# The prologue of a three-stage decoder block: new orders on VectorE and ScalarE, and the first batch's latents split by these two engines from two PSUM banks

## The chip, the core and the metric

One core of one Trainium2 chip runs the whole program in one launch. Its engines run unsynchronized and wait for each other on semaphores: TensorE (PE; its weight loads are the column PEld), VectorE (DVE), ScalarE (ACT), GpSimd (POOL), and SyncE (SP), which issues most DMAs. Each takes its instructions strictly in the order in which the program lists them. The metric is the device time of one execution, in microseconds (us); lower is better.

## The reference, cut to what matters

Inputs are x, 16 batches of 256 tokens by 256 features, and a context of 16 by 77 by 256. Three blocks follow each other, each with a residual and a plain layer norm:

```
x = LN(x + mixer(x))           # h = x@in_w+b; causal conv of 4 taps; silu; xp = h@xp_w+b
                               # a = exp(-exp(xp[:16])); b = silu(xp[16:]) * sum(h)
                               # state = state*a + b, scanned over 256 tokens; out = state@out_w+b
x = LN(x + xattn(ctx, x))      # ln = LN(x)*g+b;  q = ln@Wq;  k, v = concat(LN(ctx)*g+b, ln)@Wkv
                               # 8 heads of 128; softmax over 77+256 keys; out = heads@Wo + bo
x = LN(x + experts(x))         # top 2 of 8 experts, capacity 512 each, 256 -> 512 -> 256
```

All is float32. A product that needs more precision than one pass gives is made from operands split in a rounded high part (`_hi`) and the rest (`_lo`): three matmuls, hi·lo, lo·hi and hi·hi (helper `three`, L611 to L613).

## The kernel before

The first stage treats the 16 batches one after the other, in a loop over 8 heads in which the mixer, the norms and the projections of the neighbouring batches are laid between the attention steps of this one. The second stage runs the experts. What is changed is the prologue: the function `first()` of each engine (its name on PE, ACT, DVE, POOL and SP), which fills the pipeline before batch 0. All orders are written out by hand; every wait is a semaphore with a constant. There is no planner.

In the prologue:

- SP loads the inputs: x transposed for batches 0 and 1 (`xts`, `full`), weights, and eight weight chunks of 128x1024 (`staged(c)`): chunks 0, 1 are the value weights, 2, 3 the key weights, 4, 5 the query weights, 6, 7 the output weights.
- **Weight splits.** ACT makes w_hi of every chunk (`split_hi`, L1172). w_lo of chunks 0, 1, 2, 4, 5 is DVE's (`split_lo`, L1657, semaphore w_lo_set, counting to 5), that of 3, 6, 7 POOL's (L2025, wk_lo_set).
- **The gated values' chain of batch 0.** PE `in` (L713), ACT eviction and first tap (L1076, L1124), DVE's three other taps (L1447), ACT tanh (`tanh_half`, L1165), DVE `silu` (L1458), PE `xp` (L719), ACT's four steps of `xp` (L1081 to L1087), DVE gate (L1417, L1421) and `scan` (L1495), ACT `state_hi` and DVE `state_lo` (the states split in a row block each), PE `op` (L725), DVE `mixed` (xa = x + mixer, L1526, with its statistics), POOL `powers` (L1994, inverse roots), DVE `latents` (lnp, L1546), PE `ln` (4 transposes, L743).
- **Latents.** ACT `ln` scales and shifts both halves k of the transposed latents out of one bank into `full` (L1103). Half 1 is rounded and its rest taken by DVE (`latents_hi`, L1552, L1386), half 0 by POOL (`latents_part`, L2002, L2004). kvl_set 2 says that both low parts are there.
- **Context.** Tiles of 128 context rows: DVE statistics (`context_stats`), POOL `context_norm` (x_rs L1980, cxn L1983), PE `cT` (2 transposes, L731), ACT cfull (L1096), DVE `context_hi` (L1488), POOL `context_lo` (L1989), then values `vc` (PE, ACT L1091, DVE). Tiles 0 and 1 are in the prologue.
- **Constants.** PE sums Wo's value biases (`value_bias`, L773) and bo (L805) into a bank, DVE copies it (`cvec`, L1705). oww_x is out_w in high and low rows.
- **Idle turns** (L779) are transposes of the identity into an unused bank that keep PE at work.
- After that PE makes k (needs kvl_set 2), q (needs w_lo_set 5, so the low parts of chunks 0, 1, 2, 4, 5), `vc` 1 of tile 1, v, and enters the loop with the scores of head 0.

PE's order around the places concerned is

```
xp | vc 0, vc 1 of tile 0 | cT of tile 1 | value_bias 0-2 | op | value_bias 3-7, bo |
14 idle turns | ln | vc 0 of tile 1 | k | q | vc 1 of tile 1 | v | scores of head 0
```

An instruction that waits holds back all that stands behind it on its engine.

Of the kernel before, what the change touches and what calls it, by code (L numbers as in the profile page):

```python
# [22 lines left out]
ALU = mybir.AluOpType  # L23
# [65 lines left out]
def build(nc, x, xT, ctxt, in_w, xp_w, out_w, vecs, vec16, Wq, Wkv, Wo, bo, emb, W1, W2, out):  # L89
# [8 lines left out]
    with top:  # L98
# [306 lines left out]
        def ap(t):  # L405
            return t.bitcast(F32)
# [201 lines left out]
        def _(pe):  # L608
# [167 lines left out]
            def idle_turns(n, bank):  # L776

                for _ in range(n):
                    pe.transpose(ps[:, bank, 0:P], ident[:], ident[:])  # L779

            def first():
                pe.wait_ge(const_set, 1)
                idle_turns(13, AVB)
                pe.wait_ge(inw_ld, 16)
                unit("in", 0, 0, 0, ps[:, 5, :])
                unit("in", 1, 0, 0, ps[:, 7, :])
                unit("cT", 0, 0, 0, ps[:, 6, :])
                unit("in", 0, 1, 0, ps[:, 0, :], full)
                unit("in", 1, 1, 0, ps[:, 1, :], full)
                pe.wait_ge(xpw_set, 2)  # L790
                idle_turns(22, WOB)
                unit("xp", 0, 0, 0, ps[:, 2, :])
                pe.wait_ge(w_lo_set, 2)
                pe.wait_ge(hp_set, 3)
                unit("vc", 0, 0, 0, ps[:, 0, :])
                unit("vc", 1, 0, 0, ps[:, 4, :])
                pe.wait_ge(cxf_set, 1)
                unit("cT", 0, 1, 0, ps[:, 6, :])
                pe.wait_ge(bvb_set, 1)
                value_bias(range(0, 3))  # L800
                pe.wait_ge(owx_set, 5)
                unit("op", 0, 0, 0, ps[:, 5, :])
                value_bias(range(3, H))
                pe.wait_ge(small_ld, 48)
                pe.matmul(ps[:, AVB, 0:D], ap(ones[0:1, :]), bor[:], start=False, stop=True).then_inc(cvec_mm, 1)  # L805
                pe.wait_ge(hp_set, 4)
                idle_turns(14, S0 + 1)
                pe.wait_ge(cxf_set, 2)
                unit("ln", 0, 0, 0, ps[:, 6, :])
                pe.wait_ge(inp_set, 1)  # L810
                unit("vc", 0, 1, 0, ps[:, 2, :])
                pe.wait_ge(hp_set, 2)
                pe.wait_ge(zero_set, 1)
                pe.wait_ge(wk_lo_set, 1)
                pe.wait_ge(w_lo_set, 3)
                unit("k", 0, 0, 0, ps[:, 7, :])
                pe.wait_ge(xa_set, 1)
                pe.wait_ge(w_lo_set, 5)
                unit("q", 0, 0, 0, ps[:, 5, :])
                pe.wait_ge(vcl_set, 2)  # L820
                unit("vc", 1, 1, 0, ps[:, 4, :])
                pe.wait_ge(kl_set, 1)
                unit("v", 0, 0, 0, ps[:, 7, :])
                pe.wait_ge(hp_set, 4)
# [222 lines left out]
        def _(act):  # L1047
# [112 lines left out]
            def tanh_half(b, u):  # L1160

                a = b + 1
                need(act, cv_set, 4 * a + 2 * u + 2)
                need(act, xp_mm, a)
                act.activation(th[:, 2 * u:2 * u + 2, :], cv[:, 2 * u:2 * u + 2, :], ACT.Tanh,  # L1165
                               scale=0.5).then_inc(th_set, 1)
# [8 lines left out]
            def state_hi(b):  # L1175
                need(act, ys_set, b + 2)
                need(act, op_mm, b + 1)
                for row in (0, 64):
                    act.activation(ys_x[row:row + NST, :], ys[:], ACT.Copy).then_inc(ysh_set, 1)  # L1179

            def first():
                act.wait_ge(const_set, 1)
                act.activation(warm[:], powm[:], ACT.Exp)
                act.wait_ge(bq_set, 1)
                act.wait_ge(zero_set, 1)
                for u in range(2):
                    unit("in", u, 0, 0, ps[:, 5 + 2 * u, :])
                    first_tap(0, u)
                unit("cT", 0, 0, 0, ps[:, 6, :])
                split_hi([0])  # L1190
                tanh_half(-1, 0)
                split_hi([1])
                tanh_half(-1, 1)
                split_hi([2, 3])
                unit("in", 0, 1, 0, ps[:, 0, :])
                act.wait_ge(small_ld, 48)
                unit("xp", 0, 0, 0, ps[:, 2, :])
                unit("in", 1, 1, 0, ps[:, 1, :])
                state_hi(-1)
                unit("vc", 0, 0, 0, ps[:, 0, :])  # L1200
                unit("vc", 1, 0, 0, ps[:, 4, :])
                unit("cT", 0, 1, 0, ps[:, 6, :])
                split_hi([4, 5])
                first_tap(1, 0)
                first_tap(1, 1)
                unit("ln", 0, 0, 0, ps[:, 6, :])
                split_hi([6])
                unit("vc", 0, 1, 0, ps[:, 2, :])
                unit("k", 0, 0, 0, ps[:, 7, :])
                split_hi([7])  # L1210
                unit("q", 0, 0, 0, ps[:, 5, :])
                unit("vc", 1, 1, 0, ps[:, 4, :])
                unit("v", 0, 0, 0, ps[:, 7, :])

            first()
# [168 lines left out]
        def _(dve):  # L1384
            def minus(dst, src, hi):
                return dve.tensor_tensor(dst, src, ap(hi), ALU.subtract)  # L1386
# [265 lines left out]
            def split_lo(chunks):  # L1652
                for c in chunks:
# [3 lines left out]
                    dve.scalar_tensor_tensor(out=w_lo[o], in0=staged(c), scalar=1.0 if which else QSCALE,  # L1657
                                             in1=ap(w_hi[o]), op0=ALU.mult, op1=ALU.subtract).then_inc(w_lo_set, 1)

            def first():  # L1660
                dve.wait_ge(vec_ld, 16)

                dve.tensor_scalar(vec[:, V_BQ:V_BQ + H], vec[:, V_BQ:V_BQ + H], QSCALE, None, ALU.mult).then_inc(bq_set, 1)
                dve.memset(hp[:, :, 0:TAPS - 1], 0.0)
                dve.memset(ap(pT_lo[64:96, 2, :]), 0.0).then_inc(pad_set, 1)
                for i in range(2):
                    for part in (kv_hi[i], kv_lo[i]):
                        last = dve.memset(ap(part[:, :, KEYS:KCOL]), 0.0)
                last.then_inc(zero_set, 1)
                context_stats(0)  # L1670
                dve.wait_ge(xpr_ld, 16)
                dve.memset(xpw[:], 0.0).then_inc(xpw_set, 1)
                dve.wait_ge(xpw_set, 1)
                dve.tensor_copy(xpw[:, :, 0:NST], xpr[:, :, 0:NST])
                dve.tensor_copy(xpw[:, :, 32:32 + NST], xpr[:, :, NST:2 * NST])
                dve.memset(xpw[:, :, 64:80], 1.0).then_inc(xpw_set, 1)
                dve.wait_ge(owx_set, 2)
                dve.memset(ap(ys_x[0:32, :]), 1.0)
                dve.memset(ap(ys_x[64:96, :]), 1.0).then_inc(owx_set, 1)
                for u in range(2):  # L1680
                    for k in range(1, TAPS):
                        tap(0, 2 * u, k)
                        tap(0, 2 * u + 1, k)
                silu(0, 0)
                context_hi(0)
                context_stats(1)
                silu(0, 1)
                split_lo([0, 1])
                dve.wait_ge(oww_ld, 48)
                dve.wait_ge(owx_set, 3)  # L1690
                dve.tensor_copy(oww_x[:], oww[:]).then_inc(owx_set, 1)
                dve.wait_ge(owx_set, 4)
                minus(oww_x[64:96, :], oww[64:96, :], oww_x[64:96, :]).then_inc(owx_set, 1)
                unit("xp", 0, 0, 0, ps[:, 2, :])
                scan(-1, 1, 0)
                split_lo([2])
                state_lo(-1, 1)
                mixed(-1, 1, 0, ps[:, 5, :])
                unit("vc", 0, 0, 0, ps[:, 0, :])
                unit("vc", 1, 0, 0, ps[:, 4, :])  # L1700
                context_hi(1)
                latents(-1, 1, 0)
                split_lo([4])
                dve.wait_ge(cvec_mm, 1)
                dve.tensor_copy(cvec[:], ps[:, AVB, 0:D]).then_inc(cvec_set, 1)  # L1705
                latents_hi(-1, 1, 0)
                split_lo([5])
                unit("k", 0, 0, 0, ps[:, 7, :])
                unit("vc", 0, 1, 0, ps[:, 2, :])
                unit("q", 0, 0, 0, ps[:, 5, :])  # L1710
                dve.wait_ge(w_lo_set, 5)
                dve.memset(ap(v_lo[64:96, 2, :]), 0.0).then_inc(pad_set, 1)
# [244 lines left out]
        def _(pool):  # L1957
# [69 lines left out]
            def first():  # L2027
# [13 lines left out]
                pool.wait_ge(initr_set, 1)  # L2041
                pool.iota(initr[:, :, D], [[P, ST]], NTOK, 1, allow_small_or_imprecise_dtypes=True).then_inc(initr_set, 1)
                context_lo(0)
                context_norm(1)
                pool.wait_ge(ysl_set, 1)
                split_lo([3])
                powers(0)
                context_lo(1)
                latents_part(-1, 1)
                normalised(-1, 1)  # L2050
                split_lo([6, 7])

# [183 lines left out]
```

## Time and profile before

| what | us |
|---|---|
| median of 3 runs (lowest, highest) | 1027.61 (1026.38, 1028.1) |
| the profiled execution | 1027.42 |
| its span, first to last instruction | 1025.7 |
| PE busy in the span | 979.9 (96%) |
| DVE, ACT, POOL busy | 809.4, 729.3, 568.7 |

The span is what the trace covers; the execution's own time is 1.7 us longer. In the trace, a start is counted from the span's start, and a duration runs from an instruction's start to its end. On one engine the next instruction can start some 0.08 us before the end of the one before, so that distances between starts are a little shorter than durations. Matmuls are pipelined: their distances, not their durations, say how fast they run.

### The profile page before, as it was taken

The numbers are of one execution on the slowest core, as the hardware profiler recorded it, in microseconds if no ns is written. First come the engines' busy times: TensorE is split into PE (matmuls) and PEld (weight loads), VectorE is DVE, ScalarE is ACT, GpSimd is POOL, SyncE is SP. The second block draws the span as 40 slices with busy tenths as digits, with TensorE's granted clock in tenths as the row PEclk, the third lists the DMA queues.
The fourth block names the chain that finished last, engine by engine and source line by source line (L and its number), as shares of the span: only waits on it lengthen the run. The fifth ranks groups of instructions, "written<-read, shape, count | busy, mean of one in ns | idle before, by whom it ended". The sixth has DMA issues, their size and how long they took to land.

```text
span 1025.7 us, 21471 instructions
## 1 busy us (share of the span) xinstructions
PE 979.9 (96%) x7018; PEld 929.5 (91%) x7018; DVE 809.4 (79%) x2040; ACT 729.3 (71%) x1865; POOL 568.7 (55%) x967
## 2 busy tenths in 40 slices
PE   8999999999999999999999999999999999999960
PEld 7799999999999999999999999999999999899960
DVE  6887878887888888888888888878887877655526
ACT  6686868787777777776877787868786766365536
POOL 4743464656566556554656566545656463526543
PEclk9999999999999999999999999999999999999985
DMA  7643031213111311113110311041105110386448
GB/s 248 220 135 110 6 118 36 61 35 108 47 50 46 101 53 51 45 59 96 51 45 30 125 51 46 17 137 50 47 11 171 33 41 11 140 293 126 67 60 315
DMA packets 63829, 89.60 MB, mean 87 GB/s; under 512 B 14932, under 2 KB 44680, under 8 KB 63720
## 3 DMA queue, kind: packets, MB, share of 16 engines
q1 hardware_dynamic: 56040, 75.51, 22.8%
q0 software_dynamic: 7680, 12.72, 5.8%
q8 instruction: 58, 0.95, 0.4%
q14 instruction: 51, 0.42, 0.1%
HBM read 49.21 MB, written 38.99 MB: 86 GB/s over the span
## 4 chain that ended last, share of the span: by engine, by line
PE 77%; ACT 8%; DVE 6%; issue 3%; DMA 3%; POOL 1%; SPq 0%; ACTq 0%; DVEq 0%; POOLq 0%
PE ps L611 20%; PE ps L612 20%; PE ps L613 20%; PE ps L640 7%; PE ps L719 3%; DVE nmx L1800 2%; DMA accd<-yo,tku 1%; ACT fx L1378 1%; PE ps L655 1%; PE ps L757 1%; PE ps L657 1%; POOL accd L2174 1%; ACT hp L1076 1%; ACT ys_x L1179 1%; ACT prob L1237 1%
## 5 line engine op out<-in xcount | busy, mean ns | idle before, releaser
L2085 POOL TENSOR_SCALAR prob<-prob,rinv 128x333 f32<-128x333 f32 x256 | 144.4, 575 | 242.1 <-DVE rinv L1809 241.1
L1232 ACT ACTIVATE oT_hi<-ps 128x256 fp32r<-128x256 f32 x126 | 48.5, 385 | 151.4 <-PE ps L657 151.4
L611 PE MATMUL ps<-kv_lo,w_hi 128*128 128x256 f32 (+1 forms) x512 | 154.4, 302 | 1.1 <-DVE kv_lo L1386 1.1
L613 PE MATMUL ps<-kv_hi,w_hi 128*128 128x256 f32 (+1 forms) x512 | 153.4, 300 | 0.0
L612 PE MATMUL ps<-kv_hi,w_lo 128*128 128x256 f32 (+1 forms) x512 | 153.1, 299 | 0.0
L1237 ACT ACTIVATE prob<-ps,nmx 128x333 f32<-128x333 f32 x256 | 135.0, 538 | 7.4 <-DVE nmx L1800 7.4
L1386 DVE TENSOR_TENSOR pT_lo<-ps,pT_hi 128x512 fp32r<-128x512 f32 x254 | 131.8, 550 | 1.1 <-ACT pT_hi L1249 0.3
L1800 DVE TENSOR_REDUCE nmx<-ps 128x2 f32<-128x666 f32 x128 | 108.3, 846 | 9.3 <-PE ps L613 7.9
L640 PE MATMUL ps<-ident,prob 128*128 128x128 f32 (+1 forms) x768 | 105.5, 272 | 1.8 <-POOL prob L2085 1.0
L611 PEld LDWEIGHTS ps<-kv_lo,w_hi 128*128 128x128 f32 x512 | 96.9, 189 | 1.6 <-issue 1.5
L612 PEld LDWEIGHTS ps<-kv_hi,w_lo 128*128 128x128 f32 x512 | 96.5, 189 | 0.0
L613 PEld LDWEIGHTS ps<-kv_hi,w_hi 128*128 128x128 f32 x512 | 96.6, 189 | 0.0
L640 PEld LDWEIGHTS ps<-ident,prob 128*128 128x128 f32 (+1 forms) x768 | 90.1, 140 | 6.2 <-issue 1.6
L1447 DVE SCALAR_TENSOR_TENSOR cv<-hp,vec,cv 128x256 f32<-128x256 f32 x192 | 87.7, 475 | 1.8 <-ACT cv L1124 1.8
L611 PE MATMUL ps<-k_lo,q_hi 128*128 128x334 f32 x256 | 81.0, 317 | 1.9 <-DVE k_lo L1392 1.9
L1392 DVE SCALAR_TENSOR_TENSOR k_lo<-ps,vec,k_hi 128x334 fp32r<-128x334 f32 x128 | 71.6, 559 | 12.2 <-ACT k_hi L1055 11.7
L612 PE MATMUL ps<-k_hi,q_lo 128*128 128x334 f32 x256 | 81.0, 317 | 0.0
L613 PE MATMUL ps<-k_hi,q_hi 128*128 128x334 f32 x256 | 80.6, 315 | 0.0
L611 PE MATMUL ps<-w_lo,oT_hi 128*128 128x256 f32 x254 | 77.5, 305 | 0.2 <-DVE oT_lo L1386 0.2
L2174 POOL DMA_INDIRECT accd<-yo,tku x32 | 52.4, 1637 | 45.4 <-ACT yo L1322 20.0
L1249 ACT ACTIVATE pT_hi<-ps 128x512 fp32r<-128x512 f32 x127 | 77.1, 607 | 0.4
L1972 POOL DMA_INDIRECT slots<-xrow,slot_u x60 | 63.4, 1057 | 21.4 <-issue 20.3
(308 smaller groups left out, 3284.6 us busy)
## 6 DMA issues: line engine op xcount, KB each, us to landing
wraw<-in_W SPq DMA_DIRECT2D x14, 512.0 KB, 7.9
vcd_hi<-vst_hi SPq DMA_DIRECT2D x10, 512.0 KB, 2.7
vcd_lo<-vst_lo SPq DMA_DIRECT2D x10, 512.0 KB, 3.5
v_hi<-vcd_hi SPq DMA_DIRECT2D x32, 154.0 KB
v_lo<-vcd_hi SPq DMA_DIRECT2D x32, 154.0 KB
slots<-initr SPq DMA_DIRECT2D x8, 520.0 KB, 7.8
xs<-in_x SPq DMA_DIRECT2D x16, 256.0 KB, 4.4
xts<-in_xT SPq DMA_DIRECT2D x15, 256.0 KB, 4.1
```

Of the source, the lines that this page charges most:

```text
L611: pe.matmul(dst, hi1, lo2, start=first, stop=False, skip_group_check=True)
L612: pe.matmul(dst, lo1, hi2, start=False, stop=False, skip_group_check=True)
L613: return pe.matmul(dst, hi1, hi2, start=False, stop=last, skip_group_check=True)
L640: last = pe.transpose(ps[0:r, far if j == 2 else T0, (j % 2) * S + t * P:(j % 2) * S + t * P + P], prob[:, ring, t, j * P:j * P + r], iden ...
L1237: act.activation(prob[:, h % 2, t, 0:KEYS], ps[:, S0 + t, 0:KEYS], ACT.Exp, bias=nmx[:, h % 2, t:t + 1], accum_out=rsum[:, h % 2, t:t + 1] ...
L1249: act.activation(pT_hi[:, 0:2, :].rearrange("p j s -> p (j s)"), ps[:, T0, :], ACT.Copy).then_inc(pTh_set, 1)
L1386: return dve.tensor_tensor(dst, src, ap(hi), ALU.subtract)
L1392: dve.scalar_tensor_tensor(out=k_lo[:, idx % 2, :], in0=g[:, 0:KCOL], scalar=vec[:, V_BK + idx:V_BK + idx + 1], in1=ap(k_hi[:, idx % 2, :] ...
L1447: op = dve.scalar_tensor_tensor(out=cv[:, ct, :], in0=hp[:, ct, k:k + S], scalar=w, in1=cv[:, ct, :], op0=ALU.mult, op1=ALU.add)
L1800: dve.tensor_reduce(nmx[:, h % 2, :], ps[:, S0:S0 + NT, 0:KEYS], AX.X, ALU.max, negate=True).then_inc(nmx_set, 1)
L1972: pool.indirect_dma_start(slots, bass.IndirectOffsetOnAxis(slot_u[:, 2 * t + c:2 * t + c + 1], 0), rows[:, t, :], None).then_inc(sc_done, 16)
L2085: pool.tensor_scalar(prob[:, h % 2, t, 0:KEYS], prob[:, h % 2, t, 0:KEYS], rinv[:, h % 2, t:t + 1], 1.0, ALU.mult, ALU.mult).then_inc(norm ...
```

## The change

PE, ACT, DVE and POOL get other orders in `first()`; the latents of batch 0 get functions of their own. Half 0 of the transposed latents goes to bank 6, half 1 to bank 1. ACT makes the high part of each half directly out of its bank. DVE makes `full` of each half out of the same bank, half 1 first, and both low parts. Semaphores keep the two engines from reading one bank at the same time: DVE reads bank 1 first and ACT bank 6, then they change.

```diff
 PE first():
+            def first_latents():
+                pe.wait_ge(lnp_set, 2)
+                for k in range(KD):
+                    for t in range(NT):
+                        last = pe.transpose(ps[:, 6 - 5 * k, t * P:(t + 1) * P],
+                                            lnp[:, t, k * P:(k + 1) * P], ident[:])
+                last.then_inc(ln_mm, 1)
                 unit("vc", 1, 0, 0, ps[:, 4, :])
-                pe.wait_ge(cxf_set, 1)
-                unit("cT", 0, 1, 0, ps[:, 6, :])
                 pe.wait_ge(bvb_set, 1)
                 value_bias(range(0, 3))
...
                 pe.matmul(ps[:, AVB, 0:D], ap(ones[0:1, :]), bor[:], start=False, stop=True).then_inc(cvec_mm, 1)
+                pe.wait_ge(cxf_set, 1)
+                unit("cT", 0, 1, 0, ps[:, 6, :])
                 pe.wait_ge(hp_set, 4)
-                idle_turns(14, S0 + 1)
+                idle_turns(10, S0 + 1)
                 pe.wait_ge(cxf_set, 2)
-                unit("ln", 0, 0, 0, ps[:, 6, :])
+                first_latents()
 ACT first():
+            def first_latents():
+                act.wait_ge(ln_mm, 1)
+                act.wait_ge(zero_set, 1)
+                for k in range(KD):
+                    if k:
+                        act.wait_ge(kvh_set[1], 1)
+                    act.activation(kv_hi[0][:, k, 0:S], ps[:, 6 - 5 * k, 0:S], IDN,
+                                   bias=vec[:, V_BL + k:V_BL + k + 1],
+                                   scale=vec[:, V_GL + k:V_GL + k + 1]).then_inc(lnf_set, 1)
                 tanh_half(-1, 0)
+                tanh_half(-1, 1)
                 split_hi([1])
-                tanh_half(-1, 1)
-                split_hi([2, 3])
                 unit("in", 0, 1, 0, ps[:, 0, :])
+                split_hi([2])
...
                 state_hi(-1)
+                split_hi([3])
...
                 split_hi([4, 5])
-                first_tap(1, 0)
-                first_tap(1, 1)
-                unit("ln", 0, 0, 0, ps[:, 6, :])
+                first_latents()
                 split_hi([6])
                 unit("vc", 0, 1, 0, ps[:, 2, :])
+                first_tap(1, 0)
                 unit("k", 0, 0, 0, ps[:, 7, :])
                 split_hi([7])
                 unit("q", 0, 0, 0, ps[:, 5, :])
                 unit("vc", 1, 1, 0, ps[:, 4, :])
+                first_tap(1, 1)
 DVE first():
+            def first_latents():
+                dve.wait_ge(ln_mm, 1)
+                for k in (1, 0):
+                    if k == 0:
+                        dve.wait_ge(lnf_set, 1)
+                    dve.tensor_scalar(full[:, k, 0:S], ps[:, 6 - 5 * k, 0:S], vec[:, V_GL + k:V_GL + k + 1],
+                                      vec[:, V_BL + k:V_BL + k + 1], ALU.mult, ALU.add).then_inc(kvh_set[k], 1)
+                for k in (1, 0):
+                    dve.wait_ge(kvh_set[k], 1)
+                    dve.wait_ge(lnf_set, k + 1)
+                    minus(kv_lo[0][:, k, 0:S], full[:, k, 0:S], kv_hi[0][:, k, 0:S]).then_inc(kvl_set, 1)
                 silu(0, 0)
                 context_hi(0)
-                context_stats(1)
                 silu(0, 1)
                 split_lo([0, 1])
-                (wait for oww; oww_x copy, oww_x minus)
                 unit("xp", 0, 0, 0, ps[:, 2, :])
                 scan(-1, 1, 0)
-                split_lo([2])
+                context_stats(1)
                 state_lo(-1, 1)
                 mixed(-1, 1, 0, ps[:, 5, :])
                 unit("vc", 0, 0, 0, ps[:, 0, :])
                 unit("vc", 1, 0, 0, ps[:, 4, :])
                 context_hi(1)
                 latents(-1, 1, 0)
-                split_lo([4])
+                split_lo([2])
                 cvec
-                latents_hi(-1, 1, 0)
-                split_lo([5])
+                first_latents()
+                split_lo([4, 5])
                 unit("k", 0, 0, 0, ps[:, 7, :])
 POOL first():
                 context_lo(0)
+                (wait for oww; oww_x copy, oww_x minus, wait for both)
                 context_norm(1)
                 pool.wait_ge(ysl_set, 1)
                 split_lo([3])
                 powers(0)
                 context_lo(1)
-                latents_part(-1, 1)
                 normalised(-1, 1)
                 split_lo([6, 7])
```

Lines in brackets, and the line cvec, stand for the instructions that they name.

## Rows read from the trace of the kernel before

**Rows 1.** Busy time by stretch: us, then busy (instructions) of each engine, PEclk, DMA
```profile
46.00:48.00 2.00, 1.43 (x9) 1.06 (x8) 2.00 (x6) 1.96 (x6) 1.47 (x3) 1.00 1.05 337
...
60.00:80.00 20.00, 19.29 (x136) 18.24 (x135) 15.71 (x39) 16.87 (x44) 12.09 (x14) 1.00 0.16 44
...
993.50:994.00 0.50, 0.00 (x0) 0.00 (x0) 0.00 (x0) 0.00 (x0) 0.20 (x1) 0.82 0.00 0
```

**Rows 2.** Timeline of PE: start, us, line, operation, out<-in, count [idle before <-releaser]
```profile
17.17 1.95 PE L719 MATMUL ps<-th,xpw 128*80 128x256 f32 x8 [1.21 <-DVE th L1458]
...
22.30 0.38 PE L731 MATMUL ps<-ident,cxn 128*128 128x128 f32 x2
...
23.64 0.57 PE L725 MATMUL ps<-oww_x,ys_x 96*128 96x256 f32 x2
...
26.30 0.69 PE L805 MATMUL ps<-bor,ones 1*128 1x256 f32 x2
...
28.82 0.63 PE L743 MATMUL ps<-ident,lnp 128*128 128x128 f32 x4
...
31.95 0.39 PE L611 MATMUL ps<-kv_lo,w_hi 128*128 128x334 f32 x1 [1.11 <-DVE kv_lo L1386]
...
32.96 0.33 PE L611 MATMUL ps<-kv_lo,w_hi 128*128 128x256 f32 x1
...
37.21 0.32 PE L611 MATMUL ps<-k_lo,q_hi 128*128 128x334 f32 x1
```

**Rows 3.** Timeline of DVE in the prologue
```profile
9.79 4.94 DVE L1447 SCALAR_TENSOR_TENSOR cv<-hp,vec,cv 128x256 f32<-128x256 f32 x12 [1.76 <-ACT cv L1124]
...
16.43 0.68 DVE L1458 SCALAR_TENSOR_TENSOR th<-th,cv 128x512 f32<-128x512 f32 x1
17.03 2.35 DVE L1657 SCALAR_TENSOR_TENSOR w_lo<-staging,w_hi 128x1024 fp32r<-128x1024 f32 x2
...
21.25 0.68 DVE L1495 TENSOR_TENSOR_SCAN ys<-dec,inp 16x256 f32<-16x256 f32 x1
...
24.25 0.69 DVE L1526 TENSOR_TENSOR xa<-ps,xs 128x512 f32<-128x512 f32 x1 [0.75 <-PE ps L725]
...
27.32 0.28 DVE L1488 CAST cx_hi<-cfull 128x256 fp32r<-128x256 f32 x1
27.52 1.15 DVE L1546 TENSOR_SCALAR lnp<-xa,a_mv,a_rs 128x256 f32<-128x256 f32 x2
28.59 1.21 DVE L1657 SCALAR_TENSOR_TENSOR w_lo<-staging,w_hi 128x1024 fp32r<-128x1024 f32 x1
29.73 0.41 DVE L1705 COPY cvec<-ps 128x256 f32<-128x256 f32 x1
...
31.62 1.21 DVE L1657 SCALAR_TENSOR_TENSOR w_lo<-staging,w_hi 128x1024 fp32r<-128x1024 f32 x1
```

**Rows 4.** Timeline of ACT in the prologue
```profile
15.10 0.62 ACT L1165 ACTIVATE th<-cv 128x512 f32<-128x512 f32 x1
...
23.82 0.81 ACT L1096 ACTIVATE cfull<-ps,vec 128x128 f32<-128x128 f32 x2
```

**Rows 5.** Timeline of POOL in the prologue
```profile
23.58 2.38 POOL L2025 TENSOR_TENSOR w_lo<-staging,w_hi 128x1024 fp32r<-128x1024 f32 x1 [3.06 <-DVE ys_x L1386]
26.29 1.02 POOL L1994 TENSOR_TENSOR a_rs<-a_vv,powm 128x4 f32<-128x4 f32 x1 [0.34 <-DVE a_vv L1538]
...
31.41 3.65 POOL L2012 TENSOR_SCALAR x<-xa,a_mv,a_rs 128x256 f32<-128x256 f32 x2
```

**Rows 6.** Single tiles: count, duration in ns least/median/most, first and last start
```profile
L1980 POOL TENSOR_TENSOR x_rs<-x_vv,powm x10: 551/578/955, 6.8 to 739.2; 128x1 f32<-128x1 f32 x10
L1983 POOL TENSOR_SCALAR cxn<-cxs,x_mv,x_rs x10: 1213/1236/2785, 7.5 to 740.0; 128x256 f32<-128x256 f32 x10
...
L1386 DVE TENSOR_TENSOR kv_lo<-full,kv_hi x16: 646/648/849, 30.9 to 825.2; 128x256 fp32r<-128x256 f32 x16
...
L1103 ACT ACTIVATE full<-ps,vec x32: 553/560/567, 29.5 to 819.9; 128x256 f32<-128x256 f32 x32
```

More of the change, by code:

```diff
@@ L1685, in first @@
                 context_hi(0)
-                context_stats(1)
                 silu(0, 1)
                 split_lo([0, 1])
[L1689 to L1693, printed above, removed]
                 unit("xp", 0, 0, 0, ps[:, 2, :])
                 scan(-1, 1, 0)
-                split_lo([2])
+                context_stats(1)
                 state_lo(-1, 1)
@@ L2043, in first @@
                 context_lo(0)
+                pool.wait_ge(oww_ld, 48)
+                pool.wait_ge(owx_set, 3)
+                pool.tensor_copy(oww_x[:], oww[:]).then_inc(owx_set, 1)
+                pool.wait_ge(owx_set, 4)
+                pool.tensor_tensor(oww_x[64:96, :], oww[64:96, :], ap(oww_x[64:96, :]),
+                                   ALU.subtract).then_inc(owx_set, 1)
+                pool.wait_ge(owx_set, 5)
                 context_norm(1)
```

## Prediction

> **What bounds the kernel now.** I read busy time by stretches first [rows 1]: in the batches TensorE (PE) is at work for 19.29 of 20 us, the next engine for 16.87, so the prologue moves the end only by when it lets PE go on. The change touches only the prologue, the first 38 us. PE's rows there [rows 2] show the two places where it stood for lack of data: xp at 17.17, which waited for the gated values (silu, 16.43 + 0.68 [rows 3]), and k at 31.95, which waited for the low parts of the latents. From k on PE ran without a hole: q at 32.96, vc 1 of tile 1, v, the first scores at 37.21, and from there the batches. So the question is narrow: when does q start. It needs the low parts of weight chunks 0, 1, 2, 4 and 5, all from VectorE (DVE); the last ends at 31.62 + 1.21 = 32.83 [rows 3] and q starts at 32.96. That wait is hidden, because k ends at about the same moment; it is the one to watch.
>
> The profiled execution took 1027.42 us, 1.7 more than its span of 1025.7; the median of three is 1027.61. A shift in the span goes one for one into both; I put it on the median.
>
> **Part 1: the gated chain.** tanh 1 no longer stands behind the split of chunk 1 on ScalarE (ACT). It needs the last tap, 9.79 + 4.94 = 14.73 [rows 3], and takes 0.62 [rows 4]: ends 15.4 instead of 15.72. On DVE the statistics of context 1, which with their wait for a DMA held silu 1 until 16.43, are gone from in front of it: silu 1 starts at 15.45. Gain 0.98, and xp on PE, its four ACT steps, gate and scan move by as much: scan from 21.25 to 20.27 [rows 3]. DVE is free for them: splits 0 and 1 (2.35, now 16.06 to 18.4) start early by the same 0.98, and the oww pair (0.8 between 19.30 and 20.12) goes to POOL, which has over 3 us of slack for it. vc 0 of tile 0, which waited for split 1 (17.03 + 2.35 = 19.38 [rows 3]), starts at 18.45 for 19.44.
>
> On PE cT of context 1 (22.30 [rows 2]; two transposes, some 0.2 until the biases began) leaves the place ahead of the value biases: the op matmuls move from 23.64 to 22.44. They need the low state: DVE now puts the context statistics (20.87 to 21.71) ahead of it, so it ends at 22.05, in time. Their loads are no wait: the biases ahead of them, which began at 22.5 without one, read the load queued last. So xa starts at 23.05 for 24.25 [rows 3], and the attention norm's variances are out at 25.0 for 26.2: **1.2 us gained.**
>
> **Part 2: where that gain goes.** lnp (the latents before scaling) needs two more things in DVE's queue and POOL's.
> (a) context_hi(1) stands ahead of it and needs cT(1). PE now issues that after cvec: cvec's matmul moves from 26.30 to 25.10 and takes 0.69, so cT is at 25.73 to 26.11; ACT's pair (0.81 [rows 4]) ends at 26.98, where before it ended at 24.63 and nobody waited. DVE stands from 26.2 to 27.03, then 0.20 of cx_hi: lnp at 27.23.
> (b) POOL's powers. Context norm 1 can now start only at 21.8 (x_rs 0.55, cxn 1.21 when undisturbed [rows 6]), ending 23.7; split 3 behind it takes 2.38, to 26.05, and powers 1.02 [rows 5]: ready at 27.08. Disturbed by DVE, x_rs took 0.95, which would put lnp at 27.5.
> So lnp starts at 27.23 for 27.52: of 1.2 us 0.3 are left. The first latents' transposes follow at 28.5 for 28.82 [rows 2]. The idle turns (10 for 14, 0.125 each) end at 27.2 and hide nothing.
>
> **Part 3: the new latents on DVE, and q.** From lnp's start at 27.23, by distances between starts in [rows 3]: 1.07 to split 2 (formerly at 21.86, beside ACT's work, now here), 1.14 to cvec, 0.33 to the first new one, full[1] from PSUM at 29.77. No row has it; I take cvec's 0.41, the same 128x256 from PSUM. ACT's high part of k=1 follows it (the order by kvh_set and lnf_set), 0.56 [rows 6] with 0.04 for each handover: lo[1] can start at 30.82. DVE makes full[0] meanwhile. Then lo[1] and lo[0], both on DVE. The kv_lo row [rows 6] has 0.65 in the median of 16 and 0.85 at 31 us, with POOL at work beside it; a 128x256 from PSUM takes 0.41. I take 0.65: the second ends at 30.82 + 0.57 + 0.65 = 32.04, against 31.70 before. k follows 0.25 later, at 32.3: **0.3 late.**
> Behind them come **both** query splits, 4 and 5, where before only 5 was left: 31.96 + 1.14 + 1.21 = 34.31, and q at 34.44 for 32.96. **+1.48.** With undisturbed low parts (0.42) it is 33.98, +1.02; with 0.85, +1.85; x_rs disturbed adds 0.3. k (about 1 us) ends near 33.3, so PE then stands for 1.1 us.
>
> Edits that I cost at nothing: split_hi 3 behind state_hi (its only user, POOL, takes it at 23.7; it is out at 22.8); first taps of batch 1 behind vc (DVE takes them at about 42; v's eviction may come a little late, hidden behind the first maximum); POOL's latents gone, so that x1 and splits 6, 7 start up to 3 us earlier, where nobody waits. If DVE's splits hold POOL up instead, that lead is what covers it; without it each us more would hold up the first normalisation of batch 0, for which POOL was ready only half a us ahead. On SP, the store of tile 0's values comes 1 us earlier, and next_context(2), the first v loads and the clearing writes, which wait for split 5 or the memset behind q_lo, come later with q; what needs them is later as well.
>
> After q nothing waits: from 34.44 on all PE rows keep their distances and the first scores come at 38.7. Forecast: **+1.5, 1029.1 us.**
>
> **A rule weighed.** POOL's x1 used to start at 31.41; it now starts right behind context_lo(1), at 28.2, just before DVE's split 2. The pair to compare is x1 at 31.41 and split 5 at 31.62 [rows 3, 5], 0.2 behind it: the split took 1.21, as the undisturbed one at 28.59, and x1 took 3.65 for two. So DVE went first and POOL paid. The Trainium skill (SBUF — State Buffer, Who interferes with whom) says that a VectorE instruction with two SBUF inputs and a GpSimd instruction that reads SBUF exclude each other, and that the one issued first blocks the other for its whole length. By that, split 2 would stand until x1's first half is over. The trace agrees that they exclude each other, but not on who pays.
>
> **Rivals.**
> A. Batch 0 takes it back, and a little more (not slower). PE has holes there that hang on DVE's queue: 0.57 in 46 to 48 us and 0.71 in 60 to 80 [rows 1]. If ACT and POOL, which enter the batch less loaded, close both, 1.28, the end is +1.48 − 1.28 = +0.2, and with undisturbed low parts (+1.02) −0.3: 1027.3. It decides from where the holes closed add up to more than q's delay. Against it: the hole at 46.3 lies behind DVE's own taps, whose list is unchanged. 0.17.
> B. POOL holds DVE up: x1's first half, (3.65 − 1.21) / 2 = 1.22, keeps split 2 waiting for 1.1, and lnp's successors with it: +2.6, 1030.2. It decides from where the first half of x1 is issued ahead of split 2. For it: DVE's kv_lo at 31 us took 0.85 where its median is 0.65 [rows 6]. Against it: split 5 at 31.62. 0.17.
> C. TensorE's clock. At 46 to 48 us, with its hole, the granted clock is 1.00 (2.4 GHz), and behind the hole of 1.1 before k the matmuls keep their pace [rows 1, 2]. The last matmul is at 991.8; in the half microsecond from 993.5 the grant is 0.82 [rows 1], a fall to 0.50 (1.2 GHz) at about 993.8, so after 2.0 us without work. PE will stand 1.3 at 27.2, 1.7 at 30.6 and 1.1 at 33.3 with little between. If the clock falls to 1.2 GHz there, the work from q to the first scores (37.21 − 32.96 = 4.25) can take up to twice as long: up to 4.25 on top; I take 2.5, so 1031.6. For it: three holes in 7 us are more than in any stretch before. Against it: none is as long as 2.0. 0.08. The Trainium skill (TensorE: Matmul & The Clock Gate, Part 1) speaks for it: by it the array runs at half rate unless it has lately been kept busy.
> D. The gain of part 1 survives: lnp does come near 26.3 since cT or powers are early in a way that the queues don't show, and q at 33.5, +0.5, 1028.1. 0.05.
> Forecast, with its own range from +0.8 to +2.1 (1028.4 to 1029.7): 0.53.
>
> **How the numbers follow.** What a measurement can tell from no change is about 0.2%, 2.06 us; the forecast is below that. Slower by more: all of C, three quarters of B, an eighth of the forecast's own case: 0.08 + 0.12 + 0.07, 0.27. Faster by more: only the far end of A and what the three times of before leave open (they lie 1.7 apart): 0.09. Same: 0.64. Range 1026.7 to 1031.5: A's better end to C's middle.
>
> **What would show it.** Right: xa near 23.0; cT(1) on ACT at 26.2 and a hole on DVE before cx_hi; powers ending near 27.1; lnp at 27.2; k at 31.8 to 32.4; a hole of 1 us on PE before q, q waiting for a w_lo of DVE at 34.0 to 34.8; first scores at 38.2 to 39. Wrong: xa not before 24 (part 1 fails); lnp before 26.8 (part 2); q before 33.5 or its wait gone (part 3); split 2 starting 1 us after lnp's end (B); L611 matmuls of q at 0.24 distance instead of 0.12 (C); scores 1.5 late but the end not (A).

## The result and the profile after

| | before | changed |
|---|---|---|
| median of 4 runs each (lowest, highest), us | 1027.86 (1026.38, 1028.27) | 1034.3 (1033.73, 1035.27) |
| changed / before, 95% interval | | 1.0064 [1.0052, 1.0075] |
| the profiled execution, us | 1027.42 | 1035.27 |
| its span | 1025.7 | 1033.5 |
| PE busy; DVE, ACT, POOL busy | 979.9; 809.4, 729.3, 568.7 | 982.2; 811.7, 730.0, 575.4 |

The change costs 6.4 us. A second set of six runs against its own runs of before gave 1034.63 to 1027.85, 1.0069 [1.0056, 1.0081]. The prediction was +1.5 (1029.1, range to 1031.5): too low by 5, and outside its range.

The first silu on DVE starts between 13.44 and 14.91 us in the thirteen traces of this document, and the whole prologue moves with it. (TensorE's first `in` begins between 4.88 and 5.34 in them and takes 3.72 to 5.22.) So below, "from silu 0" is the distance to the start of that silu (14.64 before, 14.29 in the changed kernel), which stands ahead of all that was changed.

| from silu 0, us | before | forecast | changed |
|---|---|---|---|
| xa | 9.61 | 8.41 | 9.19 |
| lnp | 12.88 | 12.59 | 13.39 |
| first transpose of the latents (`ln`) | 14.18 | 13.86 | 14.68 |
| k | 17.31 | 17.7 | 18.61 |
| q | 18.32 | 19.80 | 23.96 |
| first scores | 22.57 | 24.06 | 30.96 |

Two steps carry 7.1 of the 8.4 us: k to q (1.01 before, 5.35 now) and q to the scores (4.25, now 7.00). The timeline of PE in the changed kernel (columns as in [rows 2], to which these lines answer):

```profile
15.84 1.95 PE L719 MATMUL ps<-th,xpw 128*80 128x256 f32 x8 [0.23 <-DVE th L1479]
18.84 0.50 PE L611 MATMUL ps<-w_lo,cx_hi 128*128 128x512 f32 x1 [1.05 <-DVE w_lo L1678]
...
26.16 0.44 PE L731 MATMUL ps<-ident,cxn 128*128 128x128 f32 x2
...
28.97 0.63 PE L786 MATMUL ps<-ident,lnp 128*128 128x128 f32 x4 [1.28 <-DVE lnp L1567]
...
32.90 0.39 PE L611 MATMUL ps<-kv_lo,w_hi 128*128 128x334 f32 x1 [1.90 <-DVE kv_lo L1407]
...
38.25 0.55 PE L611 MATMUL ps<-kv_lo,w_hi 128*128 128x256 f32 x1 [4.20 <-issue]
39.03 0.41 PE L611 MATMUL ps<-kv_lo,w_hi 128*128 128x256 f32 x1
...
45.25 0.32 PE L611 MATMUL ps<-k_lo,q_hi 128*128 128x334 f32 x1
```

The view puts the 4.20 ahead of q down to "issue", that is, it found no releaser. The timeline of DVE names it: q needs all five low parts, and the two splits behind the low latents took 5.59 us where two take 2.35 [rows 3]. They end at 38.15, 0.1 ahead of q.

```profile
23.48 0.69 DVE L1547 TENSOR_TENSOR xa<-ps,xs 128x512 f32<-128x512 f32 x1 [1.43 <-PE ps L725]
...
25.21 1.03 DVE L1558 TENSOR_SCALAR a_vv<-a_mv 128x2 f32<-128x2 f32 x1
...
27.68 1.14 DVE L1567 TENSOR_SCALAR lnp<-xa,a_mv,a_rs 128x256 f32<-128x256 f32 x2
28.75 1.21 DVE L1678 SCALAR_TENSOR_TENSOR w_lo<-staging,w_hi 128x1024 fp32r<-128x1024 f32 x1
...
31.89 0.76 DVE L1407 TENSOR_TENSOR kv_lo<-full,kv_hi 128x256 fp32r<-128x256 f32 x2 [0.69 <-ACT kv_hi L1197]
32.56 5.59 DVE L1678 SCALAR_TENSOR_TENSOR w_lo<-staging,w_hi 128x1024 fp32r<-128x1024 f32 x2
```

The timeline of POOL, with x1's two halves and its two last splits in a row each, says what ran beside them:

```profile
15.26 1.11 POOL L2017 TENSOR_TENSOR cx_lo<-cfull,cx_hi 128x256 fp32r<-128x256 f32 x1 [5.20 <-DVE cx_hi L1509]
16.33 1.38 POOL L2074 CAST oww_x<-oww 96x256 fp32r<-96x256 f32 x1
...
23.88 2.35 POOL L2053 TENSOR_TENSOR w_lo<-staging,w_hi 128x1024 fp32r<-128x1024 f32 x1
26.39 1.03 POOL L2022 TENSOR_TENSOR a_rs<-a_vv,powm 128x4 f32<-128x4 f32 x1 [0.17 <-DVE a_vv L1559]
...
28.66 2.31 POOL L2040 TENSOR_SCALAR x<-xa,a_mv,a_rs 128x256 f32<-128x256 f32 x1
...
30.97 1.22 POOL L2040 TENSOR_SCALAR x<-xa,a_mv,a_rs 128x256 f32<-128x256 f32 x1
...
32.27 1.51 POOL L2044 TENSOR_TENSOR x<-x,cvec 128x512 f32<-128x512 f32 x1
33.75 3.33 POOL L2053 TENSOR_TENSOR w_lo<-raw,w_hi 128x1024 fp32r<-128x1024 f32 x1
...
37.03 3.35 POOL L2053 TENSOR_TENSOR w_lo<-raw,w_hi 128x1024 fp32r<-128x1024 f32 x1
```

and DVE's splits 0, 4 and 5, for 1.21 undisturbed [rows 3], with the gate that stands behind split 1:

```profile
15.70 1.76 DVE L1678 SCALAR_TENSOR_TENSOR w_lo<-staging,w_hi 128x1024 fp32r<-128x1024 f32 x1
...
18.83 0.82 DVE L1438 SCALAR_TENSOR_TENSOR gt<-th,ut 16x256 f32<-16x256 f32 x1
...
32.56 2.30 DVE L1678 SCALAR_TENSOR_TENSOR w_lo<-staging,w_hi 128x1024 fp32r<-128x1024 f32 x1
...
34.79 3.36 DVE L1678 SCALAR_TENSOR_TENSOR w_lo<-staging,w_hi 128x1024 fp32r<-128x1024 f32 x1
```

Read them as one queue for a single thing. Split 4 stands until POOL's sum of x1 is over at 33.78, then runs its 1.1 to 34.86. POOL's split 6 (2.4 by itself) stands until then and runs to 37.1; DVE's split 5 stands behind it and runs to 38.15; POOL's split 7 stands behind that and runs to 40.4. Each pays for the one before.

Last, busy time by stretch of the changed kernel (columns as in [rows 1]):

```profile
28.00:30.00 2.00, 1.03 (x7) 0.97 (x8) 2.00 (x4) 1.70 (x3) 2.00 (x2) 1.00 0.84 342
30.00:32.00 2.00, 0.99 (x5) 0.47 (x3) 1.31 (x4) 1.42 (x3) 2.00 (x2) 1.00 0.45 182
32.00:34.00 2.00, 1.10 (x6) 0.92 (x6) 2.00 (x3) 1.76 (x4) 1.92 (x3) 1.00 0.02 4
34.00:36.00 2.00, 0.06 (x1) 0.00 (x0) 2.00 (x2) 1.49 (x2) 2.00 (x1) 0.51 0.00 0
36.00:44.00 8.00, 5.75 (x20) 5.10 (x21) 4.89 (x6) 1.09 (x3) 4.38 (x2) 0.50 0.16 49
44.00:46.00 2.00, 2.00 (x11) 1.77 (x10) 0.12 (x1) 1.88 (x4) 0.00 (x0) 0.93 0.30 104
```

The granted clock is 0.50 (1.2 GHz of 2.4) from 34.0 to about 44.2, so q, vc 1 and a part of v run at half speed: the matmuls of q behind its first took 0.41 (39.03 above) and stood 0.21 apart, for 0.28 and 0.12 at full clock.

### The profile page after: what moved, and what is told of

Its sections match the earlier page's. It is cut to its first block, busy times and chain, and to the rows that moved or that the text cites. A ratio compares the mean times of both kernels' runs of the same rounds, so it can differ in the third digit from the quotient of the medians.

```text
span 1033.5 us, 21467 instructions
## 1 busy us (share of the span) xinstructions
PE 982.2 (95%) x7014; PEld 931.6 (90%) x7014; DVE 811.7 (79%) x2040; ACT 730.0 (71%) x1865; POOL 575.4 (56%) x967
## 4 chain that ended last, share of the span: by engine, by line
PE 73%; ACT 8%; DVE 6%; issue 6%; POOL 4%; DMA 3%; SPq 0%; ACTq 0%; DVEq 0%; POOLq 0%
PE ps L611 19%; PE ps L612 18%; PE ps L613 18%; PE ps L640 7%; POOL accd L2208 4%; DMA accd<-yo,tku 3%; PE ps L719 3%; DVE nmx L1828 1%; ACT fx L1399 1%; PE ps L655 1%; PE ps L657 1%; PE ps L757 1%; ACT hp L1085 1%; ACT ys_x L1188 1%; DVE cv L1468 1%
## 5 line engine op out<-in xcount | busy, mean ns | idle before, releaser
L1421 DVE SCALAR_TENSOR_TENSOR q_lo<-ps,vec,q_hi 128x256 fp32r<-128x256 f32 x128 | 55.8, 477 | 26.8 <-ACT q_hi L1072 26.8
```

## The experiments

**Theory.** Three things add up: DVE's longer queue ahead of q (the forecast's +1.5); POOL's tensor_tensors, which now run beside DVE's splits 4 and 5 and hold them up; and TensorE's clock. Rivals: the clock does it nearly alone; the queue does it nearly alone, so that taking POOL away changes nothing; what POOL does is harmless, as I had read [rows 5]. All ratios are to runs of before on the same chip.

**POOL behind DVE's splits.** One line, which takes POOL's x1, its sum and splits 6 and 7 out of the way of splits 4 and 5:

```diff
                 context_lo(1)
+                pool.wait_ge(w_lo_set, 5)
                 normalised(-1, 1)
                 split_lo([6, 7])
```

> The changed kernel, but POOL starts x1 of batch 0 (and splits 6, 7 behind it) only when VectorE's five splits are done; nothing else is moved. Theory (q late by 5.3 us, of which about 3.8 because VectorE's splits 4 and 5 took 5.6 us for 2.4 beside POOL's two-input instructions, and TensorE at half clock from 34.0 to 44.2 us, 2.75): splits 4 and 5 take 1.2 us each, the low parts 0.42 to 0.65, q starts at 34.3 to 35.0. If the clock fell because of the single hole of 4.2 us behind k, the grant stays at 1.00 and the end is +1.5 to +2.2 over the kernel before; if it fell because of the thin stretch from 27 to 34 us, it falls again at about 34 and the end is +4 to +5. Rival (VectorE's queue is simply too long, POOL has no part): q at 38 again and +6.5.

**More idle turns.** 20 ahead of the latents, 14 between vc 0 and k, 34 between k and q, POOL as in the change:

> The changed kernel with more idle turns on TensorE: 20 for 10 ahead of the latents' transposes, 14 behind vc of tile 1, 34 behind k; VectorE, ScalarE and POOL as in the changed kernel. Theory: the grant stays at 1.00 throughout, q still starts at about 38.2 with splits 4 and 5 at 5.6 us, and from q to the first scores it takes 4.25 us for 7.0: end of the profiled span 2.7 us below that of the changed kernel, about +5.2 over the kernel before. Rival (the slow matmuls behind q come from something else than lack of work, such as the operands' arrival): 7.0 us from q to the scores again, no gain.

**Both**, with 6 turns between k and q:

> The changed kernel with both: POOL's x1 behind VectorE's splits, and idle turns on TensorE (20 ahead of the latents, 14 behind vc of tile 1, 6 behind k). Theory: the two causes add up, q at 34.3 to 35.0 and grant 1.00, first scores 4.25 us behind q, end +1.5 to +2.2 over the kernel before, which is what the order of VectorE's queue alone costs. Rival (a third cause behind the two): more than +3.

Measured, with the changed kernel's second set and a second one of the turns (the distances are those of each set's own traced execution):

| kernel | median (runs) | ratio, 95% | k, q, scores from silu 0 |
|---|---|---|---|
| changed, second set | 1034.63 (6) | 1.0069 [1.0056, 1.0081] | 18.56, 23.93, 30.71 |
| POOL behind | 1030.63 (8) | 1.0028 [1.0017, 1.0038] | 18.69, 20.72, 25.76 |
| turns | 1033.22 (4) | 1.0045 [1.0028, 1.0061] | 18.58, 23.97, 28.26 |
| turns, again | 1032.52 (5) | 1.0045 [1.0031, 1.0058] | 18.60, 24.00, 28.28 |
| both | 1029.78 (10) | 1.0013 [1.0003, 1.0023] | 18.57, 20.69, 24.97 |

DVE's splits with POOL behind them, in the timeline of that kernel, are undisturbed (2.35 for two), and q follows them at once, but at half speed, for the granted clock fell all the same, from about 32.9 to about 36.3:

```profile
32.16 2.35 DVE L1678 SCALAR_TENSOR_TENSOR w_lo<-staging,w_hi 128x1024 fp32r<-128x1024 f32 x2
```
```profile
34.62 0.55 PE L611 MATMUL ps<-kv_lo,w_hi 128*128 128x256 f32 x1 [0.27 <-issue]
```
```profile
30.00:32.00 2.00, 0.61 (x3) 0.18 (x1) 1.32 (x4) 1.61 (x3) 0.00 (x0) 1.00 0.25 100
32.00:34.00 2.00, 1.41 (x6) 1.37 (x6) 2.00 (x3) 1.36 (x3) 0.00 (x0) 0.72 0.01 4
34.00:36.00 2.00, 1.73 (x8) 1.41 (x7) 1.55 (x3) 1.48 (x2) 1.38 (x2) 0.50 0.13 38
36.00:38.00 2.00, 2.00 (x13) 1.83 (x12) 0.17 (x2) 0.84 (x2) 1.92 (x2) 0.92 0.52 158
```

With the turns the clock stays at 1.00 throughout, q is as late as in the changed kernel, and the scores follow it after 4.29:

```profile
34.00:36.00 2.00, 2.00 (x19) 1.99 (x18) 2.00 (x2) 1.68 (x3) 2.00 (x2) 1.00 0.00 0
```

So three terms come apart. All of the change but POOL's x1, sum and last splits beside DVE's, at full clock ("both"), is 0.0013 of the time, 1.3 us, with an interval from 0.3 to 2.4; DVE's longer queue is in it, and so is what POOL does to splits 0 and 1. POOL in the way of the splits at full clock ("turns" less "both") is 1.0045 − 1.0013, 3.3 us; the trace has 23.97 − 20.69 = 3.28. The clock ("changed" less "turns, again", on one chip) is 1.0069 − 1.0045, 2.5 us (2.1 between the two medians); the traces have 7.00 − 4.29 = 2.7 for the first sets and 6.78 − 4.28 = 2.5 for the second. Neither rival that names one cause alone stands: taking POOL away leaves 2.9 us, keeping the clock leaves 4.6.

The clock's share is not a fixed price. Without POOL in the way of the splits, and with q as early as in "both", its fall cost 25.76 − 24.97 = 0.8 in the trace with POOL behind and 27.52 − 24.97 = 2.5 in that of the kernel with x1 first, below; it lasted 3.4 and 6.8 us there, and 10.2 in the changed kernel. In the ratios it is 1.5 with POOL behind, in whose eight executions the mean granted clock varies from 0.981 to 0.985.

**Which of POOL's instructions.** POOL waits only before splits 6 and 7, so the sum of x1 still runs beside split 4:

```diff
                 normalised(-1, 1)
+                pool.wait_ge(w_lo_set, 5)
                 split_lo([6, 7])
```

> The changed kernel, but POOL waits for VectorE's five splits only ahead of its splits 6 and 7; x1 and its sum stay where they were. Theory (a POOL instruction with two SBUF inputs that is issued first keeps a VectorE instruction with two SBUF inputs waiting to its end): split 4 starts behind x1's sum and takes 2.3 us for 1.2, split 5 takes 1.2 for 3.4; q 2.2 us earlier than in the changed kernel against k (3.2 us behind k for 5.35), end +3 to +4. Rival (the sum alone is what holds the splits up, or splits 6 and 7 alone): both splits at 1.2 and q as with POOL's x1 behind the splits, or split 5 still at 3.4.

1032.91 (4 runs), 1.0050 [1.0034, 1.0065]. DVE's first of the two splits, then both, and POOL's sum beside the first:

```profile
32.49 2.30 DVE L1678 SCALAR_TENSOR_TENSOR w_lo<-staging,w_hi 128x1024 fp32r<-128x1024 f32 x1
...
32.49 3.43 DVE L1678 SCALAR_TENSOR_TENSOR w_lo<-staging,w_hi 128x1024 fp32r<-128x1024 f32 x2
```
```profile
32.20 1.52 POOL L2044 TENSOR_TENSOR x<-x,cvec 128x512 f32<-128x512 f32 x1
```

The sum of x1 costs 3.43 − 2.35 = 1.08, POOL's last splits the other 5.59 − 3.43 = 2.16; by the rows of the changed kernel that is split 6, since split 7 came behind split 5. q came at 21.77 from silu 0, 2.19 sooner than in the changed kernel, yet the scores only at 28.17: the clock fell here too (0.50 in every stretch from 34 to 40), and the end is above the +3 to +4 that I had expected.

**x1 ahead of the low parts.** I had read from [rows 5] that a VectorE instruction gets in ahead of x1. Here POOL holds x1 back until DVE's last `full` (the same place as the first diff, with `pool.wait_ge(kvh_set[0], 1)`), so that x1's first half is under way when DVE's two low parts of the latents come.

> The changed kernel, but POOL starts x1 (a tensor_scalar with one SBUF input, 1.22 us alone) when full of half 0 is there, at about 31.1 us, while VectorE waits for ScalarE; VectorE's low part of half 1 (two SBUF inputs) comes 0.7 us later into the running POOL instruction. If any running POOL instruction that reads SBUF holds VectorE's two-input instructions up, the low part ends 0.27 us or more behind the end of x1's first half, at 32.6 or later, and lasts 0.7 us or more. If only POOL's instructions with two inputs do (as the oww subtraction of the kernel before, 0.50 us beside a running cxn, suggests), it lasts 0.42 to 0.5 us.

One run, 1032.37; POOL and DVE, in their timelines:

```profile
30.95 1.23 POOL L2040 TENSOR_SCALAR x<-xa,a_mv,a_rs 128x256 f32<-128x256 f32 x1 [2.63 <-DVE full L1687]
...
30.95 4.53 POOL L2040 TENSOR_SCALAR x<-xa,a_mv,a_rs 128x256 f32<-128x256 f32 x2 [2.63 <-DVE full L1687]
```
```profile
31.52 0.76 DVE L1407 TENSOR_TENSOR kv_lo<-full,kv_hi 128x256 fp32r<-128x256 f32 x2 [0.68 <-ACT kv_hi L1197]
32.20 2.35 DVE L1678 SCALAR_TENSOR_TENSOR w_lo<-staging,w_hi 128x1024 fp32r<-128x1024 f32 x2
```

x1's first half began 0.57 ahead of DVE's low parts, and neither took longer: 1.23 and 0.76 for two. Its second half had to let both splits by (4.53 − 1.23 = 3.3, for 1.22). A tensor_scalar of POOL, then, held up no split and no low part of the latents here, whether or not it began first; the changed kernel has it too: x1's first half began 0.09 ahead of split 2, and the split took 1.21. What held DVE up by more than 0.3 us in these traces were POOL's tensor_tensors. Its instructions with one input cost less, but not always nothing: split 1 took 1.41 beside the cast of oww above, for 1.21 without it, and in the kernel with oww on POOL below, the low state took 0.67 beside the context norm, a tensor_scalar, for 0.42 in the changed kernel. q came at 20.66 as with POOL behind all of it, but the clock was at half from about 33.5 to 40.3, and the scores came at 27.52.

**The old order of DVE's splits in the new kernel.** Split 2 ahead of state_lo again, 4 behind lnp, 5 behind the new latents, and nothing else undone. POOL's x1, sum and splits stay as early as in the change:

```diff
                 context_stats(1)
+                split_lo([2])
                 state_lo(-1, 1)
...
                 latents(-1, 1, 0)
-                split_lo([2])
+                split_lo([4])
                 cvec
                 first_latents()
-                split_lo([4, 5])
+                split_lo([5])
```

> The changed kernel with only VectorE's split order undone: split 2 ahead of the low state, 4 behind lnp, 5 behind the new latents. Theory: one split instead of two stands between the low parts and q; it starts at about 32.9 beside POOL's x1 sum and split 6 and takes 1.2 to 3.4 us, so q at 34.3 to 36.4, and the clock falls or not with the work since 27 us: +1.5 to +5. Rival (the order of the splits has no part, since POOL blocks in any case until its splits 6 and 7 are done at 40): q at 38 or later, +6.5.

1028.49 (10 runs), 1.0003 [0.9993, 1.0013]. Its DVE and POOL timelines, then PE's:

```profile
33.08 1.22 DVE L1678 SCALAR_TENSOR_TENSOR w_lo<-staging,w_hi 128x1024 fp32r<-128x1024 f32 x1
```
```profile
33.22 2.23 POOL L2045 TENSOR_TENSOR x<-x,cvec 128x512 f32<-128x512 f32 x1
```
```profile
33.42 0.39 PE L611 MATMUL ps<-kv_lo,w_hi 128*128 128x334 f32 x1 [1.48 <-DVE kv_lo L1407]
...
34.43 0.33 PE L611 MATMUL ps<-kv_lo,w_hi 128*128 128x256 f32 x1
```

One split is left at the dangerous place, it begins 0.14 ahead of the sum of x1, and now the sum pays (2.23; with POOL behind the splits it took 1.29). q stands directly behind k, the clock stays at 1.00, and the loss is gone but for what a measurement can't tell: the trace has q 1.49 later from silu 0 than before, the medians 0.3 (−0.7 to 1.3). I had expected +1.5 to +5. So POOL's early start costs what it costs only together with the new split order, which leaves two splits behind the low parts instead of one.

**Before without its 14 idle turns**, to see whether the turns hold the clock there:

> The kernel before without the 14 idle turns ahead of the latents' transposes. TensorE then stands from about 27.0 to 28.8 and again 1.1 us from 30.8. If such a thin stretch is enough to lower the grant, it falls to 0.50 between 29 and 34 us and the end is +1 to +3; if it takes as much lack of work as in the changed kernel (from 27 to 34 us at half load), the grant stays at 1.00 and the time is that of the kernel before within 0.5 us. I expect the second: in the run with the old split order TensorE stood for 1.5 us twice and kept its grant.

1027.85 (10 runs), 1.0006 [0.9996, 1.0015], as expected; the clock stayed at 1.00 with a hole of 1.81 ahead of `ln` and one of 1.11 ahead of k:

```profile
28.00:30.00 2.00, 0.68 (x5) 0.69 (x6) 2.00 (x4) 0.99 (x3) 0.83 (x1) 1.00 0.63 258
30.00:32.00 2.00, 1.34 (x6) 0.75 (x4) 1.56 (x4) 2.00 (x4) 1.30 (x3) 1.00 0.65 266
32.00:34.00 2.00, 1.55 (x11) 1.51 (x12) 1.33 (x2) 0.83 (x2) 2.00 (x1) 1.00 0.03 8
```

**Part 1 alone, on the kernel before.** Both take from the change ACT's order (but for one first tap), the 10 idle turns, and silu 1 and splits 0 and 1 ahead of the context statistics, and keep the old latents and the old place of cT. In the first the oww pair goes to POOL; in the second it stays on DVE, behind the scan, and split 2 comes behind the low state.

> The kernel before with the parts of the change that shorten the gated chain and not those that lengthen the way to q: tanh 1 ahead of split 1 on ScalarE, context statistics behind splits 0 and 1 on VectorE, the oww pair on POOL; the latents, the split order and cT's place stay as before. Theory: xa 0.7 earlier, POOL's oww pair takes back some of it since its cast and subtraction keep splits and gate waiting; q 0.3 to 0.8 earlier, end -0.3 to -0.8 us. Rival (VectorE's whole queue up to split 5 sets q, whatever the chain does): q earlier by what VectorE is relieved of and no more, 0.8 at most, or later by the waits behind POOL.

> As the kernel with oww on POOL, but the oww pair stays on VectorE, behind the scan, and split 2 comes behind the low state; POOL as in the kernel before. Theory: nothing of POOL stands in the way of VectorE's splits, so scan and xa come 0.9 earlier, powers and cx_hi too, and q 0.8 to 1.1 earlier: end -0.8 to -1.1 us. Rival (VectorE's queue up to split 5 sets q): since it carries as much work as before, q is earlier only by the idle time that it loses, 0.3 at most.

1028.89 (11 runs), 1.0015 [1.0006, 1.0024], and 1027.77 (11 runs), 1.0002 [0.9993, 1.0011]; q from silu 0 at 19.85 and 18.69, for 18.32 before. Neither gain that I had expected came: xa itself stands at 11.14 and 9.99 from silu 0, for 9.61 before. cT of context 1, which here still stands ahead of the value biases on PE, waited for the context norm on POOL (1.58 in the first, 0.61 in the second), and op and xa waited behind it. The norm is late because the statistics that it needs now stand behind DVE's splits 0 and 1, and in the first it also took 2.82 with DVE's split 2 beside it. The oww pair was done by then (the norm's x_rs waited for DVE). POOL of the first kernel, then of the second:

```profile
19.27 0.63 POOL L1976 TENSOR_TENSOR x_rs<-x_vv,powm 128x1 f32<-128x1 f32 x1 [0.29 <-DVE x_vv L1483]
20.08 2.82 POOL L1979 TENSOR_SCALAR cxn<-cxs,x_mv,x_rs 128x256 f32<-128x256 f32 x1 [0.18 <-POOL x_rs L1976]
```
```profile
19.67 1.89 POOL L1984 TENSOR_SCALAR cxn<-cxs,x_mv,x_rs 128x256 f32<-128x256 f32 x1 [0.18 <-POOL x_rs L1981]
```

So part 1 wins nothing unless cT moves behind the biases too, as it does in the change. Whether its gain would then get past lnp with the old latents, no run here shows.

## Why the prediction was wrong, step by step

- **Part 1, +1.2 gained at xa: a third of it came.** silu 1 came 0.8 behind silu 0 and xp went early, as forecast. But DVE's splits 0 and 1 took 3.09 instead of the 2.35 that I carried over: silu 1 is early now and POOL's context_lo(0) is not, so the two meet, and split 0 took 1.76 beside POOL's 1.11 above. Split 1 took 1.41 beside the cast of oww that I had moved to POOL (1.21 in the kernel that keeps it on DVE), and the gate 0.82 beside the subtraction of oww (17.79 to 19.38; the gate took 0.41 before): I had looked for the slack of POOL and not at what the pair does to DVE. vc 0, op and xa are each 0.75 late of the forecast.
- **Part 2, lnp at 27.23: the steps held, 0.8 late.** cT, its eviction and cx_hi came as laid out, and lnp is late by the 0.8 that xa lacked. POOL's split 3 came half a us behind its place from silu 0 (23.88 to 26.23), and the variances of the attention norm, a 128x2 instruction of DVE that took 0.17 before, stood behind it for 1.03, which I had not foreseen. It cost nothing: powers ended at 27.42, and cx_hi, at 27.47, was later still.
- **Part 3, from `ln` to q: the queue was right.** Forecast 5.94; with POOL out of the way ("both") 6.03. The two low parts took 0.76 together, not 0.65 each. The 0.85 before, which I kept as the upper end and gave to rival B, was a DVE instruction that met POOL's low part, as the timelines of POOL and of DVE in the kernel before show:

```profile
30.59 0.82 POOL L2004 TENSOR_TENSOR kv_lo<-full,kv_hi 128x256 fp32r<-128x256 f32 x1
```
```profile
30.87 0.83 DVE L1386 TENSOR_TENSOR kv_lo<-full,kv_hi 128x256 fp32r<-128x256 f32 x1
```

- **"POOL's latents gone, so that x1 and splits 6, 7 start up to 3 us earlier, where nobody waits": this is the step that failed.** Somebody waits: DVE, for what it shares with POOL. Before, the sum of x1 and splits 6 and 7 ran when DVE's splits were done; 3 us earlier they lie across splits 4 and 5, the two that q waits for. It cost 3.3 at full clock. It takes the new split order as well: with POOL as early and the old order the loss is gone (1.0003).
- **The rule weighed.** The Trainium skill (SBUF — State Buffer, Who interferes with whom) says that the instruction issued first blocks the other for its whole length, and that issue order decides who blocks. I set against it that x1 paid and split 5 didn't. For two instructions of two SBUF inputs each the traces agree with it: the ends of splits 4, 6, 5 and 7 above, and split 5 in the old order, 0.14 ahead of the sum of x1, where the sum paid. For x1, a tensor_scalar, they don't, and the measurement decides: 0.57 ahead of DVE's low parts it held up neither. My mistake was to let that one pair, whose GpSimd instruction is a tensor_scalar, overrule the rule for tensor_tensors too.
- **Rival B** named the right mechanism and the wrong victim: x1 before split 2 at 28.75 (which took 1.21, undisturbed) and not the sum and the splits behind it.
- **Rival C** happened, with 0.08 given to it, and its price was close (2.5 forecast; 2.1 in the medians, 2.7 in the trace). That the price is close is in part luck: with q about as close behind k as forecast (2.03 and 2.12 for 2.14) the clock cost 0.8 in one trace (POOL behind) and 2.5 in another (x1 first). I took B and C one at a time, but here both were paid together: while PE waits for DVE, its work thins too. The clock also fell without the wait that POOL causes, as those two traces show.
- **Rival A** did not happen: the scores are 8.4 later from silu 0, and the span is 7.8 longer with a first silu 0.35 sooner, so the batches gave back no more than 0.2. The hole at 46.3 is still there, at 54 to 56 us (1.41 of 2 us).
- Predicted signs that showed the failure: q's matmuls at 0.21 and, at 38.25 for 34.0 to 34.8, q itself.

In sum, to the first scores in the trace: the forecast's 1.5, 0.8 for splits 0 and 1 (together 2.4, "both": 24.97 − 22.57), 3.3 for POOL across splits 4 and 5, and 2.7 for the clock: 8.4. In the ratios the same three come to 1.3 + 3.3 + 2.5 = 7.1, the 1.0069 of the second set; they are differences of neighbouring kernels, so that they must add up to about this, and the sum proves nothing more. The traced executions put the first term a microsecond higher than the medians do. All distances from silu 0 are set against the same one trace of before, and the old split order shows a gap of the same size (1.49 against 0.3).

**Open.** What exactly makes the clock fall. A thin stretch with no long hole was enough with POOL behind the splits (1.42, 0.61 and 1.41 of each 2 us from 28), while in the kernel with the old split order it held (0.46, 1.94 and 0.58), and before without turns as well. How long it stays down differs as much: from 3.4 us (POOL behind) to 10.2 (changed), and 6.8 in the kernel with x1 first, where q came at the same distance as with POOL behind. That idle turns on PE prevented it is shown (1.00 throughout with the turns and with both); when it would come without them isn't. In all ten executions of the changed kernel the mean granted clock was 0.980 to 0.983, with the turns 0.985 or 0.986.

## What to carry to other kernels

Whether work that nobody waits for may start earlier is a question to its engine's neighbours, not only to its consumers: lay out in time each VectorE and GpSimd instruction that reads two SBUF operands (and VectorE's small ones with one, as the variances show), and when either queue moves, look where they now cross. Put those that the bottleneck waits for where GpSimd has none to issue, or make GpSimd wait: one line gave back some 4 of 7 us (1.0069 to 1.0028). And where PE's wait grows, price the clock with the wait, as one case and not as two.

## What the runs showed of the hardware that I had not expected

- The 128x2 variances on VectorE stood for 1.03 to 1.35 us behind GpSimd's 128x1024 split (2.35), where they took 0.17 before: even so small an instruction waited out what was left of the other.
- GpSimd's tensor_scalar x1 and its tensor_tensors behaved differently as neighbours: x1 ahead of VectorE's low parts by 0.57 cost neither anything (one run), while a sum or split of GpSimd under way or ahead held VectorE's split for up to 2.2 (split 5, 3.36 for 1.21).
- VectorE's instructions that read PSUM kept their times beside GpSimd: vst_lo of the changed kernel at 38.55 took 0.68 within GpSimd's split 7, and the copy of cvec 0.41 within x1.
- TensorE's clock fell to 0.50 without any stretch of 2 us without work behind it: PE was at work for half of the 6 us before 34.0.
